# 57 stages of the final blocks and the set-up are issued at other steps

## The reference

```python
for l in range(6):
    x = attention(x, None, ..., causal=True, bias, freqs) + x      # self-attention, 16 heads of 64
    x = attention(x, context, ..., causal=False, None, None) + x   # over 2048 context rows
    x = feedforward(x, ...) + x
out = layernorm(x / max(x), final_g) @ proj_w
x = x0 + out                       # y = layernorm(x) then
x = x + attn(layernorm(x))         # 16 heads of 8, causal, with its own layernorm and residual
c = in_c                           # over the 4 elements b, in order:
    f, i = sigmoid(z[b] @ wf.T + c @ uf.T + bf), sigmoid(...)
    c = f * c + i * tanh(z[b] @ wc.T + c @ uc.T + bc)
x = x + tanh(z @ wo.T + c @ uo.T + bo)
```

## Time and profile before

| | us |
|---|---|
| median of three runs | 2611.82 |
| the three runs | 2605.08, 2611.82, 2612.84 |
| profiled execution | 2607.36 |
| its span | 2605.6 |

### The profile page before, as it was taken

The page is one execution under the profiler, slowest core; times in us unless marked ns, Lnnn a source line. Parts: engine busy times, 40 slices in busy tenths (PEclk is TensorE's granted clock), DMA queues, the critical chain, the costliest instruction groups (busy, mean ns, idle before and its releaser), DMA issues.

```text
span 2605.6 us, 37962 instructions
## 1 busy us (share of the span) xinstructions
PE 2482.2 (95%) x12652; PEld 1522.6 (58%) x12652; DVE 2238.7 (86%) x4427; ACT 2042.3 (78%) x3861; POOL 604.8 (23%) x392
## 2 busy tenths in 40 slices
PE   4799999999999999999999999999999999999876
PEld 2456656656656656656666666566566566565554
DVE  6689898898898898898898898898988988988875
ACT  2588888888888888888888888888888888888531
POOL 3312312212213213213123123123122122131000
PEclk8799999999999999999999999999999999999986
DMA  3000010001001001001001001001001001000000
GB/s 129 25 9 17 25 36 17 25 9 38 25 7 46 17 9 47 9 17 52 9 17 46 9 17 52 9 17 46 9 17 52 9 17 46 9 1 26 1 1 5
DMA packets 16573, 63.56 MB, mean 24 GB/s; under 512 B 2241, under 2 KB 7410, under 8 KB 11642
## 3 DMA queue, kind: packets, MB, share of 16 engines
q1 hardware_dynamic: 16378, 61.13, 7.3%
HBM read 48.25 MB, written 0.29 MB: 19 GB/s over the span
## 4 chain that ended last, share of the span: by engine, by line
PE 58%; DVE 17%; ACT 13%; issue 8%; POOL 3%; DMA 0%; SPq 0%; ACTq 0%; DVEq 0%; POOLq 0%
PE psS L1052 16%; PE psO L1100 9%; PE psO L1101 9%; PE psO L1103 9%; ACT P L890 6%; ACT PH L887 5%; DVE PL L636 4%; PE psL L1146 3%; PE psL L1157 2%; PE psL L1052 2%; DVE back_x L709 1%; ACT qraw L909 1%; POOL back_rstd L422 1%; DVE V L686 1%; PE psA L1203 1%
## 5 line engine op out<-in xcount | busy, mean ns | idle before, releaser
L887 ACT ACTIVATE PH<-psS 128x512 fp32r<-128x512 f32 x1536 | 1009.4, 657 | 177.3 <-PE psS L1052 158.7
L636 DVE TENSOR_TENSOR PL<-P,PH 128x512 fp32r<-128x512 f32 x1536 | 1038.5, 711 | 94.5 <-ACT P L890 84.6
L890 ACT ACTIVATE P<-psS 128x512 f32<-128x512 f32 x1536 | 1009.3, 657 | 108.5 <-DVE PL L636 108.3
L1052 PE MATMUL psS<-QT,KT 128*128 128x512 f16 x3072 | 927.5, 384 | 0.5 <-ACT P L890 0.5
L1100 PE MATMUL psO<-PH,V 128*128 128x512 f32 x1536 | 876.4, 571 | 0.0
L1101 PE MATMUL psO<-PH,VL 128*64 128x512 f32 x1536 | 606.7, 395 | 0.0
L1103 PE MATMUL psO<-PL,V 128*128 128x512 f32 x1536 | 605.9, 394 | 0.1
L1052 PEld LDWEIGHTS psS<-QT,KT 128*128 128x128 f16 x3072 | 216.2, 100 | 368.4 <-issue 281.1
L1100 PEld LDWEIGHTS psO<-PH,V 128*128 128x128 f32 x1536 | 292.2, 190 | 178.0 <-ACT PH L887 9.8
L1103 PEld LDWEIGHTS psO<-PL,V 128*128 128x128 f32 x1536 | 288.1, 188 | 152.1 <-DVE PL L636 0.8
L422 POOL TENSOR_TENSOR rn<-ssc,neghalf 128x16 f32<-128x16 f32 (+2 forms) x73 | 240.7, 3298 | 347.6 <-DVE ssc L571 265.7
(11 more groups left out here) (365 smaller groups left out, 2835.0 us busy)
## 6 DMA issues: line engine op xcount, KB each, us to landing
ctx_sb<-ctxT SPq DMA_DIRECT2D x24, 1024.0 KB, 4.7
KT<-KT SPq DMA_DIRECT2D x48, 256.0 KB, 3.5
W<-wpack SPq DMA_DIRECT2D x6, 1280.0 KB, 5.3
W<-wpack SPq DMA_DIRECT2D x6, 1088.0 KB, 7.3
W<-wpack SPq DMA_DIRECT2D x6, 576.0 KB, 5.7
KT<-biasM SPq DMA_DIRECT2D x1, 1024.0 KB
W<-tail_w SPq DMA_DIRECT2D x1, 832.0 KB
P<-biasW SPq DMA_DIRECT2D x1, 512.0 KB
```

The costliest lines, as they stand in the source:

```text
L636: nc_v.tensor_tensor(PL[:, here, :], P[:, t % PSLOTS, :], PH[:, here, :], ALU.subtract).then_inc(sem("p_lo"), 1)
L887: nc_a.activation(PH[:, t % HSLOTS, :], bank, ACT.Exp, scale=SIM_SCALE).then_inc(sem("p_hi"), 1)
L890: nc_a.activation(P[:, t % PSLOTS, :], bank, ACT.Exp, scale=SIM_SCALE).then_inc(sem("ca_exp"), 1)
L1052: ins = mm(bank, keys[part], q, start=(part == 0), stop=(part == 1))
```

## The change

Only the four plans differ. No stage is added, removed or altered, and no plan entry of the front, back or core moves. The stages of the set-up, of t, u and v are listed at other steps (57 entries), or in another order at one step. What this makes of the lists:

- Set-up, VectorE: f_begin stands in front of s_bias, and s_turned in front of f_ss_sa. The other lists keep their order.
- Window t, TensorE: t0_turn_fin behind C8 (was C11), t0_proj behind C10 (C13), t0_turn_y2 directly behind b_wo (was behind C15), t0_qkv behind C17 (C16), t0_turn1 behind C36 (C35).
- Window t, VectorE: t0_largest behind C1 (C7), t1_largest in front of b_xnT (was behind C16), t0_mask0 behind C20 (C19), t0_sum0 behind t1_in at step 20 (was 25), t0_key3 at 21 (23), t0_mask2 at 22 (24), t0_sum1 at 25 (27), t0_sum2 at 28 (29), t1_key3 behind t1_mask2.
- Window t, ScalarE: t0_exp1 to t0_exp3, t0_back0, t0_back2 and t1_exp0 to t1_exp3 one or two steps later.
- Window u, TensorE: b_turn in front of u_turn_y2, b_down in front of u_turn_z. VectorE: u_largest in front of b_spread3, u_key1 in front of u_cell0, b_silu directly behind u_sum0 (was behind u_mask2). ScalarE keeps its order.
- Window v, TensorE: v_gates2 in front of v_turn_y2 (was behind v_qkv). VectorE: v_cell2 directly behind v_own (was behind v_key1), v_sum0 in front of v_key3.
- POOL keeps its order in all windows.

The diff, cut to the lines with these stages (leading blanks cut):

```diff
 PLAN_PE = {
-8: ["u_turn_fin"], 10: ["s_table"], 11: ["t0_turn_fin", "u_proj"], 12: ["f_kv2"], 13: ["f_kv3", "t0_proj"],
-14: ["b_wo"], 15: ["u_turn_y2", "t0_turn_y2"], 16: ["t0_qkv"], 18: ["f_turn_q_sa", "b_turn", "u_qkv"],
-20: ["t1_turn_fin", "f_turn_k_sa", "b_gate", "f_sn"], 21: ["t0_s0"],
-22: ["u_gates0", "u_s0", "t1_proj", "f_sk0"], 23: ["t0_s1", "u_s1", "f_sk1"], 25: ["f_sv0"],
-26: ["t0_s2", "t1_turn_y2", "u_s2", "u_s3", "u_gates1"], 28: ["t0_s3", "t1_qkv"], 29: ["u_turn0"],
-31: ["f_sv1", "b_up"], 33: ["t1_s0", "f_sk2"], 35: ["t0_turn0", "t0_turn1"], 36: ["f_sv2", "u_turn1", "t1_s1"],
...
-63: ["f_turn_q_ca", "t1_turn_z"], 64: ["b_down"],
-65: ["v_turn_fin", "v_proj", "v_turn_y2", "v_qkv", "v_gates2", "v_s0", "v_s1", "v_s2", "v_s3", "v_turn0", "v_turn1", "v_turn2", "v_turn3", "v_pv0", "v_pv1", "v_pv2", "v_pv3", "v_turn_o", "v_wo", "v_turn_z", "v_gates3"],
+7: ["u_turn_fin"], 8: ["t0_turn_fin"], 10: ["s_table", "t0_proj"], 11: ["u_proj"], 12: ["f_kv2"], 13: ["f_kv3"],
+14: ["b_wo", "t0_turn_y2"], 17: ["t0_qkv"], 18: ["f_turn_q_sa", "b_turn", "u_turn_y2", "u_qkv"],
+20: ["t1_turn_fin", "f_turn_k_sa", "b_gate", "f_sn"], 21: ["t0_s0"], 22: ["t1_proj", "f_sk0"],
+23: ["u_gates0", "u_s0", "t0_s1", "f_sk1"], 24: ["u_s1"], 25: ["f_sv0"], 26: ["t0_s2", "t1_turn_y2"],
+27: ["u_s2", "u_s3", "u_gates1"], 28: ["t0_s3", "t1_qkv"], 29: ["u_turn0"], 31: ["f_sv1", "b_up"],
+33: ["t1_s0", "f_sk2"], 35: ["t0_turn0"], 36: ["f_sv2", "u_turn1", "t0_turn1", "t1_s1"], 37: ["t0_turn2"],
+38: ["f_sk3", "t1_s2"], 40: ["t0_turn3", "t1_s3"], 42: ["u_turn2", "f_sv3", "t0_pv0", "u_turn3", "u_pv0"],
...
+59: ["t1_turn_o"], 60: ["t1_wo"], 63: ["f_turn_q_ca", "t1_turn_z"], 64: ["b_down", "u_turn_z"],
+65: ["v_turn_fin", "v_proj", "v_gates2", "v_turn_y2", "v_qkv", "v_s0", "v_s1", "v_s2", "v_s3", "v_turn0", "v_turn1", "v_turn2", "v_turn3", "v_pv0", "v_pv1", "v_pv2", "v_pv3", "v_turn_o", "v_wo", "v_turn_z", "v_gates3"],
 PLAN_ACT = {
-22: ["f_se0", "t0_exp0"], 23: ["f_se1", "u_gates0"], 24: ["u_exp0", "f_khi", "u_exp1"], 25: ["t0_exp1"],
-26: ["t0_exp2", "u_exp2", "u_gates1"], 29: ["t0_exp3", "u_exp3"], 32: ["f_se2"], 33: ["t0_back0"],
-34: ["t1_exp0"], 35: ["t0_back2", "t1_exp1"], 37: ["t1_exp2", "u_back0"], 38: ["f_se3"],
-40: ["u_back2", "t1_exp3"], 41: ["t1_back0"], 45: ["t1_back2"], 53: ["f_raw_ca", "f_sq_ca"], 55: ["f_KT"],
+22: ["f_se0", "t0_exp0"], 23: ["f_se1"], 24: ["f_khi"], 25: ["u_gates0"], 26: ["u_exp0", "u_exp1"],
+27: ["t0_exp1"], 28: ["u_exp2", "u_gates1", "t0_exp2"], 30: ["u_exp3"], 31: ["t0_exp3"], 32: ["f_se2"],
+35: ["t0_back0"], 36: ["t1_exp0"], 37: ["t0_back2", "t1_exp1", "u_back0"], 38: ["f_se3", "t1_exp2"],
+40: ["u_back2"], 41: ["t1_back0"], 42: ["t1_exp3"], 45: ["t1_back2"], 53: ["f_raw_ca", "f_sq_ca"], 55: ["f_KT"],
 PLAN_DVE = {
-0: ["s_bias", "f_begin", "f_norm_sa", "f_xnT_sa"], 1: ["e_null"], 2: ["s_null"],
-5: ["b_spread3", "b_invert3", "b_widen3", "f_V0"], 6: ["f_V1"], 7: ["t0_largest", "u_largest"], 8: ["f_ss_sa"],
-9: ["t0_final", "u_final", "b_scale3"], 10: ["s_turned", "s_table"], 11: ["f_V2", "f_unit_sa", "t0_in"],
-12: ["u_in"], 13: ["f_null", "f_V3", "t0_norm", "b_out", "t0_gain"], 14: ["u_norm"],
-15: ["t0_own", "b_xnT", "f_kss"], 16: ["u_gain", "t1_largest"], 17: ["t0_key0"],
-18: ["t0_key1", "t1_final", "f_KT_sa"], 19: ["t0_mask0"],
-20: ["t0_key2", "t1_in", "s_ready", "f_kunit", "f_snw", "e_spread0"],
-21: ["u_own", "u_key0", "t0_mask1", "t1_norm", "e_invert0"], 22: ["u_cell0", "u_key1", "f_sp0", "f_sp1"],
-23: ["u_mask0", "t0_key3", "u_key2"],
-24: ["e_widen0", "t0_mask2", "t1_gain", "e_scale0", "u_mask1", "f_spread0"], 25: ["t0_sum0", "u_key3", "u_sum0"],
-26: ["t0_mask3", "t1_own", "u_sum1", "u_mask2", "f_invert0", "b_silu"], 27: ["t0_sum1", "t1_key0", "u_mask3"],
-28: ["t1_key1", "u_sum2"], 29: ["t0_sum2", "f_widen0", "f_scale0"], 30: ["u_back1", "u_cell1", "f_spread1"],
-31: ["f_invert1", "f_widen1", "f_sp2"], 32: ["t0_sum3", "t1_mask0"], 33: ["t0_back1", "t1_key2", "t1_mask1"],
-34: ["t1_key3", "f_scale1"], 35: ["t1_mask2"], 36: ["t1_sum0"], 37: ["t0_back3", "u_back3", "u_sum3"],
-38: ["t1_mask3", "b_act"], 39: ["f_spread2", "e_spread1", "f_invert2", "t1_sum1"], 40: ["f_sp3", "t1_sum2"],
...
+0: ["u_largest", "f_begin", "s_bias", "f_norm_sa", "f_xnT_sa"], 1: ["t0_largest", "e_null"], 2: ["s_null"],
+5: ["b_spread3", "b_invert3", "b_widen3", "f_V0"], 6: ["f_V1"], 7: ["s_turned"], 8: ["f_ss_sa"],
+9: ["t0_final", "u_final", "b_scale3"], 10: ["s_table"], 11: ["f_V2", "f_unit_sa", "t0_in"], 12: ["u_in"],
+13: ["f_null", "f_V3", "t0_norm", "b_out", "t0_gain"], 14: ["u_norm"],
+15: ["t0_own", "t1_largest", "b_xnT", "f_kss"], 16: ["u_gain"], 17: ["t0_key0"],
+18: ["t0_key1", "t1_final", "f_KT_sa"],
+20: ["t0_mask0", "t0_key2", "t1_in", "s_ready", "f_kunit", "t0_sum0", "f_snw", "e_spread0"],
+21: ["t0_mask1", "t1_norm", "e_invert0", "t0_key3"],
+22: ["u_own", "u_key0", "u_key1", "f_sp0", "f_sp1", "t0_mask2"], 23: ["u_cell0"],
+24: ["u_mask0", "u_key2", "e_widen0", "e_scale0", "f_spread0", "t1_gain"], 25: ["u_mask1", "t0_sum1"],
+26: ["u_key3", "u_sum0", "t0_mask3", "t1_own", "f_invert0", "b_silu"], 27: ["u_sum1", "u_mask2", "t1_key0"],
+28: ["t0_sum2", "u_mask3", "t1_key1", "u_sum2"], 29: ["f_widen0", "f_scale0"],
+30: ["u_back1", "u_cell1", "f_spread1"], 31: ["f_invert1", "f_widen1", "f_sp2"], 32: ["t0_sum3", "t1_mask0"],
+33: ["t0_back1", "t1_key2", "t1_mask1"], 34: ["f_scale1"], 35: ["t1_mask2", "t1_key3"], 36: ["t1_sum0"],
+37: ["t0_back3", "u_back3", "u_sum3"], 38: ["t1_mask3", "b_act"],
...
-65: ["v_largest", "v_final", "v_in", "v_norm", "v_gain", "v_own", "v_key0", "v_key1", "v_cell2", "v_mask0", "v_key2", "v_mask1", "v_key3", "v_mask2", "v_sum0", "v_mask3", "v_sum1", "v_sum2", "v_sum3", "v_back1", "v_back3", "v_out", "v_cols", "v_res", "v_z", "v_cell3"],
+65: ["v_largest", "v_final", "v_in", "v_norm", "v_gain", "v_own", "v_cell2", "v_key0", "v_key1", "v_key2", "v_mask0", "v_mask1", "v_sum0", "v_key3", "v_mask2", "v_mask3", "v_sum1", "v_sum2", "v_sum3", "v_back1", "v_back3", "v_out", "v_cols", "v_res", "v_z", "v_cell3"],
 PLAN_POOL = {
-0: ["f_sa"], 1: ["s_null"], 5: ["f_rot", "f_sa_q"], 7: ["t0_fin", "u_fin"], 8: ["s_mask"], 9: ["f_low_sa"],
-11: ["t0_y"], 12: ["u_y", "t0_y2", "b_out"], 13: ["b_ff"], 14: ["u_y2", "f_kv"], 16: ["t1_fin"], 20: ["t1_y"],
-21: ["t1_y2"], 23: ["f_klow"], 26: ["f_out"], 35: ["f_ca"], 38: ["s_rows"], 40: ["f_ca_q"], 48: ["f_low_ca"],
-54: ["t0_z"], 56: ["t1_z"], 60: ["u_z"], 65: ["v_fin", "v_y", "v_y2", "v_z"],
+0: ["f_sa"], 1: ["s_null"], 5: ["f_rot", "f_sa_q"], 7: ["t0_fin", "u_fin"], 8: ["s_mask"],
+9: ["f_low_sa", "u_y"], 11: ["t0_y"], 12: ["t0_y2", "b_out"], 13: ["b_ff"], 14: ["u_y2", "f_kv"], 17: ["t1_fin"],
+21: ["t1_y"], 22: ["t1_y2"], 23: ["f_klow"], 26: ["f_out"], 35: ["f_ca"], 38: ["s_rows"], 40: ["f_ca_q"],
+48: ["f_low_ca"], 54: ["t0_z"], 56: ["t1_z"], 58: ["u_z"], 65: ["v_fin", "v_y", "v_y2", "v_z"],
```

## The result

| | before | after |
|---|---|---|
| median, us (six runs each) | 2611.41 | 2597.68 |
| lowest to highest | 2605.08 to 2612.93 | 2596.66 to 2599.68 |
| profiled execution, time and span | 2607.36, 2605.6 | 2596.66, 2594.9 |

After over before is 0.9949, with an interval of 0.9939 to 0.9959: 13.7 us less. The two profiled executions lie only 10.7 us apart; that of after is the fastest of its six.

The account below looks back on a forecast made before the run. TensorE fills the long middle; VectorE's stream decides window t up to 2463; no engine is full in u and v. Gains 4.7 + 6.1 - 0.3 + 0.1 = 10.6 us against mean 2609.3 give 2599 us, range 2590 to 2608.

Parts of the forecast that it names:

- Steps 1 to 3 and 5: Window t: t0_largest earlier, shorter TensorE waits, b_xnT's 2.93 us idle filled, full end unchanged; gain 4.7 us.
- rival C: The clock gives back more, at b_wo, v_s0 and in window t: 14.6 us, 2594.7 us; chance 0.12.
- Step 2: Window t, TensorE: t0_qkv's wait falls from 3.5 to 1.45 us, idle from 5.1 to 2.6.
- Step 4: Window t, VectorE full: 4.75 us stay unless element 0's masks or sums wait; margins 1.4 us or more.
- rival A: Window t's gain is spent on new waits, leaving 5.9 us: 2603.4 us; chance 0.24.
- Step 6: Window u: u_largest in front of b_spread3 fills VectorE's idle, so b_wo starts 3.0 us earlier.
- Step 7: Window u: TensorE turns b's rows before u's; b_xnT 3.6 us early, u_gain 3.5 us.
- Step 8: Window u: u_key1 (0.6 us) fits the 1.49 us idle before u_cell0; total so far 4.1 us.
- Step 9: Window u: b_down in front of u_turn_z starts behind u_wo, bringing v_largest 2.0 us earlier.
- Window v: First score pair at the lower clock, v_mask0 0.9 us late: -0.3 us; at the upper clock +0.5.
- B: Window u keeps only part of its gain: 8.5 us in all, 2600.8 us; chance 0.10.
- D: Slower: TensorE's clock falls inside window t's full part, ending near 2619 us; chance 0.04.

Follow-up runs that it names:

- before_again: The kernel before, unchanged, profiled once more: 2611.91 us (one run), profiled span 2610.2 us, window v 52.49 us.
- t_alone: The kernel before with the changed order in window t alone: median 2605.69 us, ratio 0.9971 against before.
- u_alone: The kernel before with the changed order in window u alone: median 2603.39 us, ratio 0.9965 against before.
- t1large_alone: The kernel before with only t1_largest moved in front of b_xnT in window t: median 2610.97 us, ratio 0.9996 against before.
- c_early: The kernel after with u_cell0's first two instructions as their own step ahead of b_out: median 2596.71 us, ratio 0.9942 against before.
- down_alone: The kernel before with only u_turn_z put behind b_down in TensorE's list: median 2609.55 us, ratio 0.9995 against before.
- best: The kernel after with u_cell0's first two instructions ahead of b_out and v_key0 in front of v_cell2: median 2592.14 us, ratio 0.9925 against before.
- v_alone: The kernel before with the changed order in window v alone: median 2612.24 us, ratio 0.9998 against before.
- key0_first: The kernel after with v_key0 in front of v_cell2 on VectorE: median 2598.65 us, ratio 0.9946 against before.

## Why the prediction was right, and where not

The forecast was 2599 us, the median is 2597.7, and the sum of 10.6 us stands against 10.7 between the profiled executions. That the two agree to 0.1 us is luck: t gave 1.7 more and v 1.7 less, u 0.4 less and the stretch ahead of t 0.6 more. The errors of v and of the stretch ahead of t lie within what two executions of one kernel differ by there. Against before_again the same profile of after has 15.3 us. What was right is the mechanism in windows t and u: their 6.4 and 5.7 us come back in t_alone and u_alone.

- *Steps 1 to 3 and 5, window t: mechanism right, size too small (4.7, measured 6.4).* b_scale3 came 2.5 us early, not 2: b_spread3 was 0.2 us late and not 0.7, since VectorE waited before no PL from t0_largest on. The replay lost another half microsecond on the way to t0_gain, which ended 2.5 us early in the trace and 1.5 in the replay. The idle time of 0.54 us before t0_own is gone, as the replay had it; t0_qkv's six products took 0.94 us in after, and 1.65 at the lower level in before. t0_key0 starts 30.57 us behind the end of block 21, not 36.60: 6.0 of the 6.4. The clock belongs to it: the 0.81 of the earlier trace rows became 1.00, which I had left to rival C. How much of the gain is the clock's no run separates.
- *Step 2.* t0_qkv's wait is 1.2 us (forecast 1.45), t0_turn_y2's 0.2 (0.85).
- *Step 4: right, but by a narrower path than it says.* There is no idle time in after before t0_mask0, t0_sum0, t0_mask2 or t0_sum1. t1large_alone shows that the wait of rival A comes if t1_largest moves alone; in after other moves of t carry it, and which of them do stays open.
- *Step 6: right.* b_wo 3.0 us earlier, at the lower clock again (3.54 us, was 3.75): the 1.8 us kept for the range didn't come.
- *Step 7: right.* b_xnT 3.8 us early against the end of block 22 (forecast 3.6), u_gain 3.75 (3.5).
- *Step 8: failed.* It took the 1.49 us in front of u_cell0 as a gap that a step of 0.6 us can fill. But u_cell0 begins with L833 and L834, and TensorE's gates, for which that very gap waits through ScalarE, need L834. What was moved in front of the cell pushed the wait along with it: it gave nothing, where 0.6 us were forecast. u_mask0 came 3.74 us early, as much as u_own, and not 4.1. c_early shows the way to fill the gap: the two instructions first.
- *Step 9: right.* 1.96 us, in after and in down_alone. v_largest stands behind u_z's wait, of 0.44 us and not over 0.5.
- *Window v: right for what it spoke of, incomplete.* The score pair ran at the lower level (2.07 us), v_mask0 started 16.23 us behind v_largest, 1.0 us late (forecast 0.9). Where the products of L1289 run at the lower level in both, the new order costs 0.2 us to v_out (34.23 against 34.04 and 34.07; forecast 0.3). Most of the rest of the 2.0 us, 1.6, are these products. In the execution shown they ran mostly at the upper level; the eight other profiles with the old order of v have them at 6.8 to 7.2 us, as after has (7.15). So it isn't the new order that slowed them. The prediction left them out of its sum: it looked for the clock at b_wo and v_s0 only.
- *Set-up.* The 0.3 us by which VectorE's first step for a tile of block 0 (L641) starts earlier (97.73, was 98.05) can't be laid to the change: before_again has 97.72 with the old order, and the profiles of the table spread over 3.6 us before window t begins. No run has these moves alone.
- *The signs named beforehand.* b_wo of u starts 3.66 us behind the last product with the values (forecast 3.7), and from there to v_largest it takes 42.7 us (42.3). One sign of being wrong came: v's first mask stage stands behind a gap, of 0.96 us. It is the term of -0.3.
- *The base.* Taking the profiled execution's 2607.4 for low was right; the cause is the clock in window v, as far as before_again stands for the typical execution. In the first group 15 of 16 runs of before lie at 2611.4 to 2615.2 (in the third, 5 of 31 lie under 2609), so the median gained 3 us more than the profiles do.

The Trainium skill ("TensorE: Matmul & The Clock Gate", Part 1) says that the clock gate's own timing runs freely and isn't reset when a kernel starts, so that the same kernel meets it at another phase from run to run; it tells this of the first products after the start. before and before_again agree in that the same kernel meets another clock, with 4.4 us between them in window v, late in the kernel; the runs don't show whether the free timing is the reason.

*The rivals.* A is refuted for the change, and shown as real for t1_largest alone. B did not happen (step 9 is whole). C happened in window t only. D, slower by a clock that falls in t, did not: 1.00 from 2404 to 2462. Other profiles with this order of t have 0.91 to 0.96 in the second part of it, and their t is as long (113.6 to 113.7 us).

*What stays open:* how often each order gets the upper level at the end of v, since only profiled executions show it, and whether best's lead beyond 1.4 us is such a case.

## What to carry to other kernels

Before a step is put into an engine's idle time, follow the wait back through the other engines to see whether it ends in an instruction behind the gap: a step that holds both the end of a wait and what the wait is for must be cut in two first. Don't take the gains of moves measured alone for their sum: in window t they gave 1.5 and 3.0 us alone, and 6.4 together with the others that came with them. And where an engine's clock has two levels, read a short stretch by starts between instructions that don't hang on it, and profile the kernel before twice: the execution shown of before was a lucky one, by 4.4 us in window v.

## What the runs showed of the hardware

The granted clock in windows u and v isn't fixed by the order of the lists. The same 25 last products took 4.9 to 5.2 us in ten profiled executions and 7.6 to 7.7 in four (v_alone, before_again, key0_first, down_alone). The products some 10 us earlier don't foretell it: those of L1289 span 7.18 us both in t_alone, whose end is fast, and in before_again, whose end is slow. The gates of window u, 12 products, took 1.8 us in the two profiles of before and 3.0 in down_alone, whose lists are the same up to there. So a difference of 2 to 4 us between two executions of this kernel can be the clock's alone. What decides the level stays open.
